# Third stage of a four-stage kernel: values made turned as the last side work, output statistics by pairs of row tiles, keys ahead of the last output tile

## The reference

```
h = norm_scale * x / (rms(x) + 1e-8) * split_scale
q = h @ Wq.T   (8 heads x 64);   k = h @ Wk.T, v = h @ Wv.T   (2 groups x 64)
attn = softmax(q k^T / 8);       out = (attn v) joined over heads
block = x + out @ Wo.T
```

## Time and profile before

| what | value |
|---|---|
| median of 3 runs | 1569.31 us (1569.26 to 1570.19) |
| profiled execution | 1568.97 us |
| its span | 1567.0 us |
| mean granted clock of TensorE | 0.979 |
| busy: PE, DVE, ACT, POOL | 93%, 65%, 52%, 47% of the span |
| third stage, first score of map 0 to first turn after map 7 | 318.6 us to 947 us of the span |

### The profile page before, as it was taken

The page is one execution under the profiler, slowest core; times in us unless marked ns, Lnnn a source line. Parts: engine busy times, 40 slices in busy tenths (PEclk is TensorE's granted clock), DMA queues, the critical chain, the costliest instruction groups (busy, mean ns, idle before and its releaser), DMA issues.

```text
span 1567.0 us, 21347 instructions
## 1 busy us (share of the span) xinstructions
PE 1453.4 (93%) x7252; PEld 1187.5 (76%) x7252; DVE 1014.7 (65%) x2044; ACT 819.9 (52%) x1574; POOL 730.3 (47%) x970
## 2 busy tenths in 40 slices
PE   5999999989999999999999996699899999999996
PEld 4888788767787878787878774577788888888874
DVE  5888789677879797988888775445332424424233
ACT  4666557578777777878787763321222213212221
POOL 4788546545454545555454444123324333243332
PEclk9999999999999999999999999799999999999998
DMA  7465023320002020202020201322011010110100
GB/s 207 130 160 135 21 95 107 108 81 1 1 10 73 1 81 2 81 1 81 1 81 1 101 1 54 111 84 67 2 54 53 1 54 0 54 54 0 54 28 27
DMA packets 46205, 88.51 MB, mean 56 GB/s; under 512 B 2720, under 2 KB 3744, under 8 KB 46112
## 3 DMA queue, kind: packets, MB, share of 16 engines
q1 hardware_dynamic: 42416, 79.98, 14.9%
q0 software_dynamic: 3696, 7.34, 2.9%
HBM read 62.14 MB, written 25.17 MB: 56 GB/s over the span
## 4 chain that ended last, share of the span: by engine, by line
PE 73%; DVE 13%; POOL 5%; issue 4%; ACT 3%; DMA 2%; SPq 0%; POOLq 0%; DVEq 0%; ACTq 0%
PE f_inner L57 23%; PE context L1629 12%; PE f_down L2055 9%; PE context L57 7%; PE score L57 5%; PE turned L1664 5%; PE score L851 4%; PE context L1692 2%; PE context L1690 2%; DVE g_ptl L1551 2%; DVE g_neg_max L1537 2%; PE turned L57 1%; DVE f_wl L1979 1%; POOL g_prob L1247 1%; PE f_inner L2027 1%
## 5 line engine op out<-in xcount | busy, mean ns | idle before, releaser
L1247 POOL TENSOR_SCALAR g_prob<-g_prob,g_inv_sum 128x512 f32<-128x512 f32 x256 | 177.7, 694 | 298.4 <-DVE g_inv_sum L1542 298.3
L57 PE MATMUL f_inner<-f_xth,f_wh 128*128 128x512 f32 x704 | 281.3, 400 | 15.4 <-DVE f_wl L1979 12.7
L57 PE MATMUL f_inner<-f_xtl,f_wh 128*128 128x512 f32 x704 | 280.0, 398 | 0.0
L1889 ACT ACTIVATE f_silu<-f_inner,f_inner_scale 128x512 f32<-128x512 f32 x88 | 60.7, 689 | 414.0 <-PE f_inner L57 414.0
L1948 DVE SCALAR_TENSOR_TENSOR f_hidden<-f_inner,f_inner_scale,f_silu 128x512 f32<-128x512 f32 x88 | 66.0, 750 | 313.8 <-PE f_inner L57 313.8
L1837 POOL TENSOR_TENSOR f_hl<-f_hidden,f_hh 128x512 fp32r<-128x512 f32 x88 | 127.9, 1453 | 297.0 <-DVE f_hh L1954 297.0
L1537 DVE TENSOR_REDUCE g_neg_max<-score 128x1 f32<-128x512 f32 x256 | 175.4, 685 | 84.0 <-PE score L57 82.8
L1368 ACT ACTIVATE g_prob<-score,g_neg_max 128x512 f32<-128x512 f32 x256 | 176.6, 690 | 95.7 <-DVE g_neg_max L1537 93.4
L1551 DVE TENSOR_TENSOR g_ptl<-turned,g_pth 128x512 fp32r<-128x512 f32 x256 | 173.9, 679 | 17.2 <-ACT g_pth L1416 15.1
L1664 PE MATMUL turned<-identity,g_prob 128*128 128x128 f32 x1024 | 156.9, 276 | 26.9 <-DVE g_ptl L1551 26.9
L57 PEld LDWEIGHTS f_inner<-f_xth,f_wh 128*128 128x128 f32 x704 | 133.3, 189 | 54.2 <-DVE f_wl L1979 17.3
(11 more groups left out here) (230 smaller groups left out, 3393.6 us busy)
## 6 DMA issues: line engine op xcount, KB each, us to landing
xt<-x_t SPq DMA_DIRECT2D x16, 512.0 KB, 6.2
x_mixed<-x_resident SPq DMA_DIRECT2D x8, 1024.0 KB, 4.3
x_pair<-x_mixed SPq DMA_DIRECT2D x8, 1024.0 KB, 8.0
g_res<-x_mixed SPq DMA_DIRECT2D x8, 1024.0 KB, 6.7
x_attended<-g_res SPq DMA_DIRECT2D x8, 1024.0 KB, 5.2
x_pair<-x_attended SPq DMA_DIRECT2D x8, 1024.0 KB, 5.6
x_resident<-x SPq DMA_DIRECT2D x7, 1024.0 KB, 10.9
factor_sum<-factors POOLq DMA_DIRECT2D x7, 1024.0 KB, 10.8
```

What stands on the lines that cost most here:

```text
L57: last = nc.tensor.matmul(out, lhsT, rhs, start=(n == 0), stop=(n == len(pairs) - 1))
L1247: nc.gpsimd.tensor_scalar(prob[:, at, :], prob[:, at, :], inv_sum[:, at:at + 1], 1.0, ALU.mult, ALU.mult).then_inc(prob_ready, 1)
```

## The change

The names come in another order, and with other places. v is no longer made in 48 short matmuls. Its place is taken by two steps. `vt`, the last name of a map, makes the values turned (128 value columns x 512 rows) in 12 matmuls of 512 columns with the v weights as the stationary operand, like k, and ACT copies it to the new tile `v_turned`. `v`, the first name of the next map, turns it back with four transposes, and then ACT and DVE write its high and low part as before. k stands ahead of wo3.

The budget of a unit becomes 8, 7 from unit 24 on, and 3 beside contexts, and what a name takes over its budget is taken from the next unit. Output statistics, scales and normalisation are done for tiles 0 and 1 together and for tiles 2 and 3 together. By the new schedule wo0 to wo3 end in units 12, 15, 20 and 24 (before 11, 13, 19, 20), ACT normalises them in units 19, 20, 28 and 29 (before 24 to 27), and POOL adds them in 20, 21, 29 and 30 (before 25 to 28). The h tiles are normalised in 5, 6, 8 and 11 (before 5, 6, 10, 11), the first two conversions of outputs are in 25 and 26 (before 20 and 24). STATS and SCALES stay.

| unit | side work before | side work after |
|---|---|---|
| 0 to 5 | q1 to q3 in 12, 12, 12 | v, q1, q2, 3 of q3 |
| 6 to 9 | h0 (7), h1 (8) | 9 of q3, h0 (7) |
| 10 to 16 | wo0, wo1, h2, h3 | h1, wo0, wo1, h2 |
| 17 to 20 | wo2, wo3 | h3, wo2, 7 of k |
| 21 to 24 | k, 24 of v | 5 of k, wo3 |
| 25 to 31 | 24 of v, q0 | q0, vt |

```diff
-NAMES = ["q1", "q2", "q3", "h0", "h1", "wo0", "wo1", "h2", "h3", "wo2", "wo3", "k", "v", "q0"]
+NAMES = ["v", "q1", "q2", "q3", "h0", "h1", "wo0", "wo1", "h2", "h3", "wo2", "k", "wo3", "q0", "vt"]
+OWN = ("v", "q1", "q2", "q3")
-H = (5, 6, 10, 11)
-CONVERT = (20, 24, 32, 39)
-SHARE, SHARE_BESIDE_OUT = 8, 4
+H = (5, 6, 8, 11)
+CONVERT = (25, 26, 32, 39)
+SHARE, SHARE_AT_END, SHARE_BESIDE_OUT = 8, 7, 3
...
-        room = SHARE_BESIDE_OUT if (u - OUT_LAG) % T < 2 else SHARE
-        while waiting and room > 0:
+        room = min(room, 0) + (SHARE_BESIDE_OUT if (u - OUT_LAG) % T < 2 else SHARE if u < 6 * T else SHARE_AT_END)
+        while waiting and room >= 0.5:
...
-NORM = [WO[-1] + 4 + t for t in range(T)]
+NORM = [WO[1] + 4, WO[1] + 5, WO[3] + 4, WO[3] + 5]
 ADD = [at + 1 for at in NORM]
+LAG = {"vt": 1}
...
-            def output_scales(b):
-                wait_alone(pool, s, ostats, b + 1)
+            def output_scales(b, i):
+                half = slice(2 * i, 2 * i + 2)
+                pool.wait_ge(ostats, 2 * b + i + 1)
...
+                elif name == "vt":
+                    last = nc.scalar.copy(v_turned[:, :], src[:, :])
...
+                if name == "vt":
+                    dve.wait_ge(side_free, side_use(b, name))
+                    dve.sem_inc(side_free, 1)
+                    return
...
-                if t == T - 1:
-                    wait_alone(dve, s, side_free, use + 1)
-                    for t in range(T):
+                if t % 2 == 1:
+                    dve.wait_ge(side_free, use + 1)
+                    for t in (t - 1, t):
...
+            def turn_v(b, use):
+                side_bank(use)
+                pe.wait_ge(side_hi, side_split(b - 1, "vt"))
+                for t in range(T):
+                    cols = slice(t * P, (t + 1) * P)
+                    last = nc.tensor.transpose(side[use % 2][:, cols], v_turned[:, cols], s.identity[:, :])
+                last.then_inc(side_ready, 1)
...
-                    if name == "v":
-                        cols = bank_cols = slice(m // (3 * T) * P, (m // (3 * T) + 1) * P)
-                        pairs = split(hth[:, k, cols], htl[:, k, cols], wvh[:, k, :], wvl[:, k, :])
-                    elif name == "k":
-                        pairs = split(wkh[:, k, :], wkl[:, k, :], hth[:, k, :], htl[:, k, :])
+                    if name in ("k", "vt"):
+                        wh, wl = (wkh, wkl) if name == "k" else (wvh, wvl)
+                        pairs = split(wh[:, k, :], wl[:, k, :], hth[:, k, :], htl[:, k, :])
...
             side_share(-1, "k", 0, 3 * T, True)
-            side_share(-1, "v", 0, 3 * T * T, True)
             pe.wait_ge(own.wq_lo, T)
             side_share(-1, "q0", 0, 3 * T, True)
+            side_share(-1, "vt", 0, 3 * T, True)
```

More of the change, by code:

```diff
@@ L1012, with side_at @@
 SHARES, END = side_schedule()
[L1013 removed]
+AHEAD = len(SPLIT) - len(OWN)
 WO = [END[f"wo{t}"] for t in range(T)]
 RESIDUAL = [at - 1 for at in WO]
[L1016 removed]
+NORM = [WO[1] + 4, WO[1] + 5, WO[3] + 4, WO[3] + 5]
 ADD = [at + 1 for at in NORM]
[L1020 to L1022 removed]
+LAG = {"vt": 1}
+assert max(END[name] + LAG.get(name, 2) for name in SPLIT) < UNITS
+def side_at(b, name):
+    return side_use(b, name) % 2
 def side_use(b, name):
@@ L1031, in side_use @@
     if isinstance(b, int) and b >= B - 1 and name[0] == "w":
-        missing = [n for n in NAMES[:j] if n[0] != "w" and (b == B or n[0] != "q")]
+        missing = [n for n in NAMES[:j] if n in SPLIT and (b == B or n not in OWN)]
         j -= len(missing) + (AHEAD if b == B else 0)
@@ L1047, in side_done @@
 def side_done(u, first, last, drain, lag):
-    return [name for name in NAMES if END[name] + lag == u and side_runs(name, first, last, drain)]
+    return [name for name in NAMES if END[name] + min(lag, LAG.get(name, lag)) == u
+            and side_runs(name, first, last, drain)]
 def side_runs(name, first, last, drain):
@@ L1055, in side_runs @@
         return not first
-    return not drain and (not last or name in ("q1", "q2", "q3"))
+    return not drain and (not last or name in OWN)
 def attention_fetch(nc, s, stack, norm_scale, split_scale, wq_t, wk_t, wv_t, wo_t, x_in):
@@ L1306, in step @@
                     residual(b - 1, 1 - p, RESIDUAL.index(u))
-                if u == WO[-1] + 2 and not first:
-                    output_scales(b - 1)
-                if u in ADD and not first:
+                for i in range(2):
+                    if u == WO[2 * i + 1] + 2 and not first:
+                        output_scales(b - 1, i)
+                if u in ADD and not first and not drain:
                     add(b - 1, ADD.index(u))
@@ L1596, in turn_h @@
                     cols = slice(k * P, (k + 1) * P)
-                    last = nc.tensor.transpose(side[side_at(f"h{t}")][:, cols], h[:, t % 2, cols], s.identity[:, :])
+                    last = nc.tensor.transpose(side[use % 2][:, cols], h[:, t % 2, cols], s.identity[:, :])
+                last.then_inc(side_ready, 1)
[5 more added lines that the diff above has]
+                    last = nc.tensor.transpose(side[use % 2][:, cols], v_turned[:, cols], s.identity[:, :])
                 last.then_inc(side_ready, 1)
@@ L1603, in side_share @@
             def side_share(b, name, start, end, done):
-                use, out = side_use(b, name), side[side_at(name)]
+                use, out = side_use(b, name), side[side_at(b, name)]
                 if name[0] == "h":
                     return turn_h(b + 1, use, int(name[1]))
+                if name == "v":
+                    return turn_v(b, use)
                 if start == 0:
@@ L1628, in side_share @@
                                  split(oh[:, k, cols], ol[:, k, cols], woh[:, k, :], wol[:, k, :]))
-                    last = nc.tensor.matmul(out[:, bank_cols], *pairs[n], start=(k == 0 and n == 0),
+                    last = nc.tensor.matmul(out[:, :], *pairs[n], start=(k == 0 and n == 0),
                                             stop=(k == T - 1 and n == 2))
```

43 lines of the change are left out of this document (22 added, 21 removed).

## The result

The changed kernel takes 1581.4 us (median of 4 runs, 1579.87 to 1582.49) against 1569.6 us of the kernel before in the same comparison, a ratio of 1.0075 with an interval of 1.0064 to 1.0087. The forecast was 1574.0: slower, as it turned out, by 11.8 us in place of 4.6. So the direction and the wide range (1560 to 1584) held, and the prediction's own case, 1569 to 1580, did not.

What follows compares the result with a forecast made beforehand. PE (93% of the span) was taken as the bound, DVE second. Five maps stalled by 3.5 us (+17.5) less 12.9 gained elsewhere gave +4.6 us on 1569.31: 1573.9, rounded 1574, range 1560 to 1584.

Steps and rivals of the forecast that it cites:

- own case: Whole kernel: a stall in maps 2 to 6 outweighs gains elsewhere; 1574 us, range 1569 to 1580, chance 0.47.
- The stall: Unit 0 of maps 2 to 6: DVE waits some 5 us for the input load behind the late store; +17.5 us.
- rival three: Disturbed maps: PE's gap also halves the clock and late scales pile up ACT work; +9 us, 1583, chance 0.15.
- the load's issue comes one unit and a half before the map's end: SP's queue at a map's end: sign in the later profile that the next input's load is issued that late.
- Rival one: Maps 2 to 6: load late, but PE not held for all of it; period 81.0 us, total 1560, chance 0.22.
- Rival two: Maps 1 to 6: no stall, load not delayed or covered; each 1.9 to 3 us shorter, 1543, chance 0.08.
- Rival four: Maps: gains halved by growing waits, stall only 4 us; 5 x 2.5 - 7 = +5.5 us, 1574, chance 0.08.
- the sum of the gains: All places outside maps 2 to 6: ahead of map 0, maps 0, 1 and 7, and after the last score; -12.9 us.
- Waits taken over: Unhindered map: PE work 73.4 us plus 4.8 of waits, near today's 4.5, gives 78.2, 1.9 less than before.
- Ahead of map 0: Chain piece before map 0: v's 48 matmuls (5.4 us) become 12 (2.8), so -2.6 us.
- Map 0 and map 7: First and last map: less PE work and side work better spread; -2.5 us (0 to -5) and -4.0 (0 to -7).
- The tail: After the last score: two adds run under the scales, power on 128x2 cheaper, two aggregates less; -1.9 us.

Runs made afterwards that it cites:

- the first experiment: Against the changed kernel, SP issues the load of the next input ahead of the store that waits for the late adds; 1553.4 us, ratio to before 0.9901.

## Why the prediction was right, and where its sizes were off

The stall was foreseen with its cause, its place and its size, and it decided the direction. The number was not: a rise of 11.8 us is two and a half times 4.6, and 1581.4 lies above the own case's 1580. It is in the range because that reaches up to rival three, and rival three was mostly wrong; to that extent it is luck.

**The stall** is shown, by taking it away, by making it in the other kernel, and by cutting its wait from 23.3 to 12.8 us. Its working holds term by term. From the reciprocal of unit 30 to the data 553.59 to 564.50, 10.9 us (10.9 put); from there to PE's unit 7 13.5 (13.6); from there to unit 30 56.7 (53.1 of work and 3.4 of waits); from there to the next reciprocal 2.6 (2.6). The two ends that the rows above lack are these, PE's units 7 and 30 and DVE's reciprocal:

```profile
578.02 0.60 PE L1687 MATMUL turned<-identity,g_prob 128*128 128x128 f32 x4
```

```profile
634.72 0.60 PE L1687 MATMUL turned<-identity,g_prob 128*128 128x128 f32 x4
```

```profile
637.29 0.15 DVE L1557 RECIPROCAL g_inv_sum<-g_row_sum 128x1 f32<-128x1 f32 x1
```

That is 83.7 round map 3's head and 83.7 on the mean of five maps, against 83.6. Against an unhindered map it is 4.8 us (78.9) and not the 5.4 that the forecast has between its 78.2 and 83.6. The sign "the load's issue comes one unit and a half before the map's end" holds by DVE's count: issued at 556.29, 3.4 us before DVE was free for it at 559.64. By PE's count the next map had begun, at 555.02. Rival one (81.0 a map) lost because DVE's slack lies behind the stall, not under it: DVE takes up the lumps one after another at full rate, and PE gets its unit 7 only then. Rival two is excluded by the 4.66 us of waiting. Rival four had one half right: it put the gains at -7 because the waits would grow, and they were -7.4. Its other half, 2.5 us more in each of five maps, was 3.6.

**Rival three came in small part.** In maps 2, 3, 5 and 6 PE's gap was followed by a stretch at half the clock. Here is the busy time of the 3.4 us of it in map 3 (clock 0.51), PE's gap being the one before 566.59 above:

```profile
566.90:570.30 3.40, 3.35 (x10) 2.25 (x9) 3.30 (x9) 2.74 (x7) 1.67 (x2) 0.51 0.01 3
```

Map 4 had none. Period less wait is 78.87 there, 78.85 and 78.87 in maps 3 and 5 with 3.4 us of it, and 79.33 and 79.45 in maps 2 and 6 with 6.8 us. So a stretch of 3.4 us cost nothing, and DVE was busy through it, as I had put against this rival. The kernel before with late adds says the same: 80.20 to 80.23 in maps 2 to 4 with such a stretch, 80.20 in map 5 at full clock. A second stretch in a row, which reaches on into the units where PE is the bound, went with 0.5 to 0.6 us more in each of two maps. In five maps that is 1.0 us, not the 8 to 10 of the rival, and the late scales that it also named left nothing in these sums. The Trainium skill, "TensorE: Matmul & The Clock Gate", section "PE-mode transpose", would have the added turns weigh on the clock. Map 1 of the changed kernel, with 148 turns, ran at 1.00, and so did map 3 once the gap was gone, so the trace does not bear it out here; a long stretch of turns alone, which would try it, is in no run.

**The step that failed is the sum of the gains**: -12.9 put, -7.4 found. That is 5.5 of the 7.2 us between forecast and result; the rest is where k starts (0.9), the stall (0.5) and the fourth stage (0.5), less 0.2.

- *Waits taken over.* "I take 4.8 us of waits" is the mis-sized term of the unhindered map: PE's work did fall by the 2.2 us that the step put (undoing it cost 2.1 us of a map's time), but map 1 is 78.9 and not 78.2, so its waits are 5.5. The pair of budgets gives the place: with 8 and 4 the map is 78.3, that is 4.9 of waits. The even spread, with the units that move by it, costs 0.5 us a map, 0.7 in map 1. Unit 0 of map 1 takes 3.64 us in the changed kernel and 2.72 with the old budgets, where vt ends in unit 27 and its copy can be done long before. Copying vt first on the even budgets brought unit 0 to 3.16 and the map only 0.2, so that the copy is the whole cause is not shown.
- *Ahead of map 0.* -2.6 was the work alone. PE then ran into a wait of 1.21 us that v's long stretch had covered: the bank of vt is freed by k's low part. With the order changed, the stretch is 2.9 us shorter than before (13.76 to 10.88), so the work's price was right and its cover was not looked for.
- *Map 0 and map 7.* 1.0 and 2.6 in place of 2.5 and 4.0. With the load ahead of the store map 0 is 1.4 shorter, map 7 2.6; both are then about what I put or better, but in that trace the stretch behind map 7 is 3.8 us longer, so that map 7 and what follows it up to the last output total gained nothing by it (97.7 us in place of 96.4). In map 0 PE's waits are the same in both traces (DVE waited 6.6 us for scores in the changed kernel and 4.9 in the other), but the changed kernel's has a stretch at half clock 57.5 us after the first score that the other lacks; that it is the cause was read, not tested. In map 7 of the changed kernel 6.8 us ran at half clock; the first experiment's map 7 has none and its drain has more.
- *The tail.* -1.3 in place of -1.9. The adds and the power came as put. But POOL's little scale operations now stand beside DVE's first two adds. In the changed kernel, pair one and pair two, on POOL and DVE:

```profile
982.07 0.23 POOL L103 TENSOR_SCALAR g_ove<-g_omv 128x2 f32<-128x2 f32 x1 [5.75 <-DVE g_omv L1511]
982.37 0.22 POOL L104 TENSOR_SCALAR g_oshift<-g_omv 128x2 f32<-128x2 f32 x1
...
987.62 0.57 POOL L103 TENSOR_SCALAR g_ove<-g_omv 128x2 f32<-128x2 f32 x1 [2.44 <-DVE g_omv L1511]
988.26 0.53 POOL L104 TENSOR_SCALAR g_oshift<-g_omv 128x2 f32<-128x2 f32 x1
```

```profile
987.45 1.26 DVE L1598 TENSOR_TENSOR g_res<-g_res,g_total 128x512 f32<-128x512 f32 x2
...
990.74 1.40 DVE L1598 TENSOR_TENSOR g_res<-g_res,g_total 128x512 f32<-128x512 f32 x2 [2.03 <-ACT g_total L1395]
```

They took 0.65 us more together, about the difference of 0.6.

**Still open**: why one unit of delay in two normalisations costs 0.75 us a map where no load waits for them, and one unit less 0.6, and which wait it is by which the old budgets do better by half a microsecond. The rows show where waits are; no run took the single one away.

## What to carry to other kernels

When a step at the end of a loop body moves later, look at what stands behind its store on the same queue: here a load for the next round, needed at once. Issuing that load first cost nothing in the kernel that had no stall and turned a loss of 0.75% into a gain of 1.0%. A stall at the head of the second engine's queue passed to the period whole, although that engine was idle for a fifth of the time; here slack that lay behind the stall did not absorb it.

Price a removed stretch of PE work together with the waits that ran under it, and test a respread of work by itself: here the turned values came to 0.3 us a map net in one order and 2.1 in another, and neither pair of kernels changes them quite alone.

## What the runs showed of the hardware

Two-column operations on POOL took 0.57 and 0.53 us while DVE ran an addition of 128x512 whose two inputs are both tiles in SBUF, the on-chip memory (`g_res` and `g_total`, L1598), and 0.23 and 0.22 us while DVE ran nothing. That DVE is busy is not enough: inside the maps the same operation took 0.24 us within DVE's subtraction at L1566, one input of which is an accumulator bank.

```profile
605.43 0.68 DVE L1566 TENSOR_TENSOR g_ptl<-turned,g_pth 128x512 fp32r<-128x512 f32 x1
...
605.79 0.24 POOL L103 TENSOR_SCALAR g_ove<-g_omv 128x2 f32<-128x2 f32 x1
```

I had priced them as in the trace of before, where DVE did nothing then.

The load of the next input took 8.2 us from its issue to the first statistics behind a store of the same size (556.29 to 564.50). The page's medians from issue to landing are 7.9 us for that load in the changed kernel and 7.8 with the load ahead of the store, but this does not acquit the store: with the load ahead, the reload of the residual, also of 1 MB, is issued 0.5 us before the load. One load of the first experiment, issued at 350.62, has no transfer beside it, and it took 5.5 us:

```profile
x_pair<-x_mixed SPq DMA_DIRECT2D x1, 1024.0 KB, 5.5
```

All nine kernels with the load ahead of the store in map 0 show 5.5 us for it, while the loads of this input beside another transfer took 7.3 to 9.9. So by an estimate from these rows some 2.7 of the 8.2 us went to the transfers beside it, the store and, from 561.17 on, the residual's reload; the rest of what the store cost was the load's place in the queue behind it. How much of the 2.7 is the store's alone is not shown.
